# Graph network with capsule routing on one core: shares ahead of the messages, flags in PSUM, half sums on GpSimd and two alternating sum buffers in routing rounds 2 to 6

## The reference

```
xk = normalize(x.reshape(n, 8, 16))          # 8 capsules of 16 features, each to length 1
z = xk[src]                                  # for every edge
u = xk
for _ in range(6):
    p = softmax(sum(z * u[trg], axis=2), axis=1)       # 8 shares of each edge
    agg = segment_sum(z * p[:, :, None], trg, n)
    u = normalize(agg.reshape(n, 8, 16) + xk)
```

## Time and profile before

| what | value |
|---|---|
| median of 3 runs | 12146.04 us (12140.96 to 12165.63) |
| the profiled execution | 12153.88 us |
| its span | 12152.0 us |
| TensorE, weight loads | 57% and 43% of the span busy |
| VectorE | 58% |
| ScalarE | 28% |
| GpSimd | 46% |
| mean granted TensorE clock | 0.713 of full speed |

### The profile page before, as it was taken

One profiled execution on the slowest core, in us unless ns is written; L12 is line 12 of the kernel. 1 busy time (PEld: TensorE's weight loads), 2 busy tenths in 40 slices (PEclk: granted clock), 3 DMA queues, 4 the chain that ended last, 5 costly groups with the idle time before them and its releaser, 6 DMA issues. The chain is left out here.

```text
span 12152.0 us, 198157 instructions
## 1 busy us (share of the span) xinstructions
PE 6929.4 (57%) x41381; PEld 5175.5 (43%) x41382; DVE 7092.0 (58%) x19002; ACT 3369.7 (28%) x10770; POOL 5647.4 (46%) x5161
## 2 busy tenths in 40 slices
PE   4444433333366666787455553555547777777775
PEld 3211112222222222444344442444437676767675
DVE  7422235454554544777544445444448888888888
ACT  0000000000100000121111111333337776777775
POOL 0466656666255554333355553555543343434342
PEclk9767765555655555998655555666669999999998
DMA  0222234444355556554122222333345454545454
GB/s 21 79 105 107 112 95 104 103 105 102 72 156 155 154 155 144 186 180 131 45 58 58 58 58 47 95 97 95 96 86 164 143 163 142 164 143 163 143 163 122
DMA packets 1108605, 1387.92 MB, mean 114 GB/s; under 512 B 277722, under 2 KB 974382, under 8 KB 1108142
## 3 DMA queue, kind: packets, MB, share of 16 engines
q1 hardware_dynamic: 955182, 1090.46, 28.7%
q0 software_dynamic: 153344, 296.65, 11.9%
HBM read 1002.58 MB, written 383.96 MB: 114 GB/s over the span
## 5 line engine op out<-in xcount | busy, mean ns | idle before, releaser
L2097 POOL TENSOR_TENSOR msg_r<-zo_r,ex_r 128x1024 f32<-128x1024 f32 x580 | 1121.6, 1934 | 1878.2 <-ACT ex_r L2184 1878.2
L2192 ACT ACTIVATE hots_r<-zo_r,tot_r 128x128 f32<-128x128 uint8 x4640 | 1416.5, 387 | 576.0 <-DVE tot_r L2137 389.4
L2225 PE MATMUL ps<-msg_r,hots_r 128*128 128x128 f32 x9280 | 1195.2, 282 | 573.9 <-ACT hots_r L2192 461.4
L2225 PEld LDWEIGHTS ps<-msg_r,hots_r 128*128 128x128 f32 x9280 | 1087.6, 193 | 681.5 <-DVE u_sum L2150 666.5
L598 POOL DMA_INDIRECT ring_e<-t_tab,st_e x880 | 831.1, 944 | 893.5 <-DVE st_e L590 597.2
L2213 PE MATMUL ps<-u,wide_r 128*128 x9280 | 1143.2, 277 | 169.2 <-ACT wide_r L2177 164.8
L1879 POOL DMA_INDIRECT z_r<-x_tab,st_r x880 | 833.9, 948 | 808.3 <-issue 441.2
L477 POOL DMA_INDIRECT rec_tab<-st_pay,st_row x832 | 808.6, 972 | 858.3 <-DVE st_pay L529 596.7
L2213 PEld LDWEIGHTS ps<-u,wide_r 128*128 128x128 f32 x9280 | 1093.8, 194 | 171.8 <-issue 171.7
L1078 POOL DMA_INDIRECT ring_m<-t_tab,st_m x880 | 842.8, 958 | 684.9 <-issue 349.4
L598 POOL DMA_INDIRECT ring<-y_tab,st x880 | 883.4, 1004 | 550.5 <-DVE st L590 290.4
(11 more groups left out here) (316 smaller groups left out, 13040.7 us busy)
## 6 DMA issues: line engine op xcount, KB each, us to landing
zo_r<-zo_tab SPq DMA_DIRECT2D x2320, 192.0 KB, 2.6
y_tab<-y_out SPq DMA_DIRECT2D x250, 512.0 KB
k_tab<-ring_m SPq DMA_DIRECT2D x220, 520.0 KB
ring_e<-k_tab SPq DMA_DIRECT2D x220, 520.0 KB
ohts_e<-oht_tab SPq DMA_DIRECT2D x440, 128.0 KB
zo_tab<-z_r SPq DMA_DIRECT2D x220, 256.0 KB
dl_b<-dl_tab SPq DMA_DIRECT2D x220, 128.0 KB
oht_tab<-ohts SPq DMA_DIRECT2D x220, 128.0 KB
```

Of the source, the lines that this page charges most:

```text
L2097: nc.gpsimd.tensor_tensor(msg[:, s % WR].rearrange("p c (k d) -> p c k d", d=CD), z_of(s).rearrange("p c (k d) -> p c k d", d=CD), ex[:, s ...
L2192: last = nc.scalar.activation(hots[:, s % WR, c, :], rows[:, c, :], ACT.Copy, scale=tot[:, s, c:c + 1])
L2225: last = nc.tensor.matmul(ps[:, 4 + s % 2, c // 2 * D:(c // 2 + 1) * D], hots[:, s % WR, c, :], msg[:, s % WR, c, :], start=c % 2 == 0, st ...
```

## The change

In later_rounds, and with small edits around it:

1. **Shares ahead of the messages.** VectorE multiplies the flagged reciprocal with the exponentials into a new tensor share; GpSimd's message multiplies z with it, and waits for it. The one-hot is no longer scaled: hot is one ScalarE instruction over all eight chunks, and waits for nothing of VectorE.
2. **Flags in PSUM.** pair_ok is copied once to PSUM banks 6 and 7. The flagged reciprocal is made from there, and written there.
3. **Half sums on GpSimd.** After the product GpSimd adds features 8 to 15 of each capsule to features 0 to 7 (fold); VectorE's reduction then reads 8 instead of 16 features.
4. **Two sum buffers.** u_sums takes turns by the round. The one not in use is reset to unit by ScalarE in ten pieces during octets 4 to 13. Both are first filled in round 1. u_sq is gone: squares are written into u. y_row and dl_f are freed ahead of the routing layer.
5. **The end of a round in parts**: squares and their sums in four parts, root, maximum, reciprocal and product in two. The first two wide matrices of a round are made in the round before.
6. **Orders.** VectorE, ScalarE, TensorE and GpSimd have new orders, zo has 6 buffers, dot, ex and tot two. SP no longer waits for widen.
7. **No loops**: all 580 octets are written out on every engine, waits are for constants, and 16 register reads stand ahead of every fourth octet.

```
                 OC = 2 * OP
-                WR = 2
+                ZR, WR = 6, 2
+                parts = [(0, 13), (13, 26), (26, 38), (38, NTP)]
...
+                    flat = ps[:, 6:8, :].rearrange("p b w -> p (b w)")
+                    RESETS = 10
+                    def inverse(g):
+                        at = 2 * NPAIR + g % 2 * OC
+                        return flat[:, at:at + OC]
...
+                    def sums_of(r):
+                        return u_sums[(r + 1) % 2]
...
+                            for g in range(rounds * NO):
+                                o = g % NO
+                                if o % 4 == 0:
+                                    places = registers([mybir.EngineType.SP], pair_at, o, NCH - 2)
+                                if g >= ZR:
+                                    sp.wait_ge(s_msg, g - ZR + 1)
+                                    sp.wait_ge(s_hot, g - ZR + 1)
...
+                            def message(g):
+                                pool.wait_ge(s_share, g + 1)
+                                if g >= WR:
+                                    pool.wait_ge(s_sum, g - 1)
+                                nc.gpsimd.tensor_tensor(
+                                    msg[:, g % WR].rearrange("p c (k d) -> p c k d", d=CD),
+                                    z_of(g).rearrange("p c (k d) -> p c k d", d=CD),
+                                    share[:, g % 2, :].rearrange("p (c k) -> p c k", k=CAPS).unsqueeze(3)
+                                    .broadcast_to([P, OC, CAPS, CD]), ALU.mult).then_inc(s_msg, 1)
+
+                            def fold(g):
+                                pool.wait_ge(s_prod, g + 1)
+                                nc.gpsimd.tensor_tensor(prod[:, :, 0:CD // 2], prod[:, :, 0:CD // 2],
+                                                        prod[:, :, CD // 2:CD], ALU.add).then_inc(s_half, 1)
+                            for r in range(rounds):
+                                for k in range(-1, NO + 1):
+                                    if k >= 1:
+                                        message(r * NO + k - 1)
+                                    if k + 1 < NO:
+                                        fold(r * NO + k + 1)
...
+                            def reduce(g):
+                                dve.wait_ge(s_half, g + 1)
+                                if g >= 2:
+                                    dve.wait_ge(s_e, g - 1)
+                                v.tensor_reduce(dot[:, g % 2, :], prod[:, :, 0:CD // 2], AX.X, ALU.add).then_inc(s_dot, 1)
...
+                            def flagged(g):
+                                dve.wait_ge(s_p, 3 * g + 2)
+                                at = g % NO * OC
+                                v.tensor_tensor(inverse(g), flat[:, at:at + OC], tot[:, g % 2, :], ALU.mult)\
+                                 .then_inc(s_p, 1)
+
+                            def shares(g):
+                                dve.wait_ge(s_p, 3 * g + 3)
+                                if g >= 2:
+                                    dve.wait_ge(s_msg, g - 1)
+                                v.tensor_tensor(share[:, g % 2, :].rearrange("p (c k) -> p c k", k=CAPS),
+                                                inverse(g).unsqueeze(2).broadcast_to([P, OC, CAPS]),
+                                                ex[:, g % 2, :].rearrange("p (c k) -> p c k", k=CAPS), ALU.mult)\
+                                 .then_inc(s_share, 1)
...
+                                    if now:
+                                        reduce(g)
+                                    if r >= 1 and k == 2:
+                                        dve.wait_ge(s_u, r * RESETS)
+                                    if behind:
+                                        add(r, late, 0)
+                                    if k + 1 < NO:
+                                        product(g + 1)
+                                    if behind:
+                                        add(r, late, 1)
+                                    if now:
+                                        total_share(g)
+                                    if behind:
+                                        add(r, late, 2)
+                                    if now:
+                                        share_inverse(g)
+                                    if behind:
+                                        add(r, late, 3)
+                                    if now:
+                                        flagged(g)
+                                        shares(g)
...
+                                for n, (a, b) in enumerate([(parts[0][0], parts[1][1]), (parts[2][0], parts[3][1])]):
+                                    dve.wait_ge(s_rt, 2 * r + n + 1)
+                                    link(v.tensor_scalar(norms(a, b), norms(a, b), 1e-12, None, ALU.max))
+                                    link(v.reciprocal(norms(a, b), norms(a, b)))
+                                    v.tensor_tensor(capsules(u, a, b), capsules(sums_of(r), a, b),
+                                                    norms(a, b).unsqueeze(2).broadcast_to([P, (b - a) * CAPS, CD]),
+                                                    ALU.mult).then_inc(s_go, 1)
...
-                                    for c in range(OC):
-                                        last = nc.scalar.activation(hots[:, s % WR, c, :], rows[:, c, :], ACT.Copy,
-                                                                    scale=tot[:, s, c:c + 1])
-                                    last.then_inc(s_hot, 1)
...
+                            def hot(g):
+                                if g >= WR:
+                                    act.wait_ge(s_sum, g - 1)
+                                nc.scalar.activation(hots[:, g % WR], hot_bytes(g, False), ACT.Copy).then_inc(s_hot, 1)
...
+                                for k in range(NO):
+                                    g = r * NO + k
+                                    exponential(g)
+                                    if k + 3 < NO or (k + 3 < NO + 2 and r + 1 < rounds):
+                                        widen(g + 3)
+                                    hot(g)
+                                    if 4 <= k < 4 + RESETS and r + 1 < rounds:
+                                        reset(r, k - 4)
...
+                                for k in range(-2, NO + 1):
+                                    g = r * NO + k
+                                    if k + 2 < NO:
+                                        if (k + 2) % 4 == 0:
+                                            tiles = registers(PE_ENGINE, pair_tile, k + 2, NT)
+                                        expand(g + 2, tiles)
+                                    if k >= 1:
+                                        total(g - 1)
```

More of the change, by code:

```diff
@@ new lines, in norms, with capsules, registers @@
+                    def norms(a, b):
+                        return nrm[:, a * CAPS:b * CAPS]
+                    def capsules(big, a, b):
+                        return big[:, a:b, :].rearrange("p t (k c) -> p (t k) c", c=CD)
+                    def registers(engine, table, o, most):
+                        return nc.values_load_multi_w_load_instructions(
+                            table[0:1, o * OP:min(o + 4, NO) * OP], engines=engine, min_val=0, max_val=most,
+                            skip_runtime_bounds_check_because="a bucket or a chunk number, bounded where the table is made")[1]
@@ new lines, in _ @@
+                            for r in range(rounds):
+                                if r >= 1:
+                                    pe.wait_ge(s_go, 2 * r)
+                                for k in range(-2, NO + 1):
[6 more added lines that the diff above has]
+                                        total(g - 1)
```

276 lines of the change are left out of this document (120 added, 156 removed).

## The result

| kernel | median, us | lowest to highest | runs |
|---|---|---|---|
| before | 12152.43 | 12140.96 to 12165.63 | 4 |
| changed | 11515.24 | 11509.13 to 11551.14 | 4 |

What follows compares the result with a forecast made beforehand. VectorE bounds the kernel at 4.81 us an octet; TensorE would then set 3.95. Octets save 494.5 us, round boundaries 45, entry to round 2 0.5: 540 less, 11606 us on the median's scale, range 11490 to 11848.

Steps and rivals of the forecast that it cites:

- the prediction's own signs of being wrong: In the trace: VectorE's waits before the reduction naming GpSimd, TensorE waiting on messages, or issue gaps every few octets.
- its first case: Routing octets: TensorE sets the period, 3.75 to 4.15 us, total 11490 to 11720 us; chance 0.70.
- TensorE's octet, 3.84: Routing octet on TensorE: the same matmuls, 4.66 less 0.82 idle, need 3.84 us.
- T = 3.80 + 0.15: Octet period: TensorE's matmuls plus its register reads, no longer under idle time, give 3.95 us.
- VectorE then wants 3.6 to 3.8: VectorE's octet after the change: 3.58 us plus up to 0.20 of register reads, at worst 3.95.
- nothing else needs as much: Routing octets: no other engine needs as much time as TensorE, so TensorE sets the period.
- Six buffers in place of four ... Nothing: Source loads by DMA: two more buffers give one or two octets of lead, no time gained.
- (a): Rival, octet loop: a cross-engine chain of message, half sum, reduction and shares sets 4.2 to 4.6 us; chance 0.22.
- the margin of 0.3: GpSimd's half sum ends at 3.3 us of VectorE's step, covered by 0.3 or more before the next reduction.
- about 21: Between routing rounds: TensorE idles about 21 us.
- (b): Rival, written-out octets: instruction fetching stalls engines; 1.1 us an octet would give 12238 us; chance 0.04.
- (c): Rival, flags' multiplication: its 0.5 us is not GpSimd's hold, so nothing gained, 12130 to 12187 us; chance 0.04.

Runs made afterwards that it cites:

- e3: Changed kernel without register reads on VectorE, bucket sums going to fixed, wrong rows: 11386.74 us, ratio 0.9384 to the kernel before.
- e4: Changed kernel with VectorE's register reads moved from ahead of the reduction to behind the product of the octet before: 11400.37 us, ratio 0.94 to the kernel before.
- e11: Changed kernel with VectorE's register reads behind the product, e4's edit again on another chip: 10392.63 us, 118 less than e10.
- e9: Changed kernel with VectorE's order of operations as in the kernel before: 10623.16 us, 112 more than e10.
- e1: Changed kernel with the flags' multiplication reading the flags from SBUF again, output still in PSUM: 11592.63 us, 77 more than the changed kernel.
- e2: Changed kernel without half sums on GpSimd, VectorE's reduction reading all 16 features: 11726.27 us, 211 more than the changed kernel.
- e8: Changed kernel with four zo source buffers in place of six: 12433.06 us, ratio 1.1169 to the kernel before, 1922 us more than e10.
- e12: Changed kernel with five zo source buffers in place of six: 10572.66 us, 62 more than e10.
- e7: Kernel before with one edit, the flags copied to PSUM once and multiplied from there: 10999.92 us, ratio 0.9882 to the kernel before.
- e10: Changed kernel itself, run again on the third chip: 10510.83 us, ratio 0.9441 to the kernel before.

## Why the prediction was right, and where it was off

**Right in sign and in the means, not in the bound.** VectorE was the bound at 4.81; the hold by GpSimd, the order, the half sums and the round's end all showed, and TensorE ended near full. The period came out 3.79 for 3.95: 575 x 0.16 = 92 of the 97 us by which the forecast of the saving was short. But TensorE alone does not set this period, and two of the prediction's own signs of being wrong stood in the trace: "issue" gaps every four octets (141.8 us) and TensorE waiting on messages (103.9). That the period still fell into the band of its first case, 3.75 to 4.15, is in part luck: TensorE's octet was taken 0.38 too long, and 0.22 of waiting for each other, which the sum did not have, made up for over half of it.

**The mis-sized term is TensorE's octet, 3.84, and with it "T = 3.80 + 0.15".** It measured 3.57. The working added 1.89 (one group's start to the next) to 1.95 (the next group's record to its end, taken from an octet in which TensorE idled behind it). Back to back both groups step by 1.79. Of the difference 0.16 is the overlap of a record's end with the next start; 0.10 is that a group behind an idle takes longer, as again here, where the sums at 9616.49 are 1.89 long to the next start. The text gave "some 0.1 less", it is 0.27. The 0.15 for TensorE's register reads was nothing: with them it is busy 99.8% of e3's stretch.

**What set 3.79 are VectorE and TensorE by turns, through a term that the text had and did not use.** "VectorE then wants 3.6 to 3.8" was 3.58 + 0.20. Measured are 3.42 + 1.03/4 = 3.68, above TensorE's 3.57 and below the period. The remaining 0.11 is VectorE waiting for the sums of a TensorE that its own read had held up: in four octets the read takes 1.03 us from VectorE, the message is late by it, TensorE loses 0.77 ahead of the sums and 0.10 in them, and 14.28 + 0.87 = 15.15, against the 15.12 of four periods. VectorE, faster than TensorE by 0.15 an octet, catches up and waits in its turn. The read was taken at the 0.8 us of the earlier trace rows's wait and is 1.0. So "nothing else needs as much" was the false sentence. Shown by e3, e4 and e11: without the exposed reads TensorE's 3.57 to 3.59 is the period and 115 to 129 us go.

**VectorE's parts.** Step 3.58 forecast, 3.42 measured. Flags 165 ns (0.20 to 0.27 as a step), shares 225, reduction 686 for 678, neighbouring sums apart: all as costed. As shares of the time they were worth less alone than in the sum, as leaving one out shows: half sums 211, order 112 (net of the reads that e9 hides), flags 77, round ends 39, shares 17, together 456 of 637. Why the rest belongs to no part alone was not taken apart. One reason shows in e1 and e2: what a part fails to save goes first into the waits for TensorE's sums, 0.11 an octet.

**"Six buffers in place of four ... Nothing" was wrong as a step.** It was read as more lead for a wait of 121.6 us. In the new order of ScalarE it decides over more than the whole gain: 1922 us without it (e8), 62 with one buffer of two (e12). The forecast did not suffer, because the change has both. What was missed is a ring through load, widen and hot; the ring examined under (a) left the loads out.

**GpSimd.** Half sum 1.27 for 1.0 to 1.2. The prediction's estimate of 1.11 us from the figure in section 3.1 of the Trainium skill's page GPSIMD Engine Reference is low as well; 1266 ns for 512 elements is more an element than the message's 1934 for 1024. By the list of waits it stayed covered, with 14.1 us of idle ahead of the reduction in all. By the starts the margin of 0.3 is gone: the half sum ends at 9613.10 + 1.27 = 9614.37, and the reduction starts at 9614.40, 0.20 behind the shares' start where e1 and e2 have 0.15. So in these octets the reduction seems to wait 0.05 for it, under the record of the shares.

**Round ends.** 45 forecast; 39 by leaving them out, and 22.1 us of idle for "about 21". A round took 10018.60 - 9546.41 = 472.2 us for the 487 forecast; 115 x 3.79 = 436 of it, so 36 for boundary and filling, against 34.

**The rivals.** (a), T 4.2 to 4.6, did not happen. Its mark, TensorE waiting on messages, showed (103.9 us), but e4 removed most of it by moving reads alone: it followed from them. (b): instructions are fetched in 387 packets, 4.6 MB, for 79 packets before, and TensorE and VectorE show no gap for it: TensorE's 99.8% in e3 leaves none. By the rule of the Trainium skill's page Runtime: NRT & Kernel Launch, section Instruction fetch mechanics, straight code is fetched ahead; the trace agrees. (c), that the hold is something else, is refuted by e1: with the input back in SBUF, and the output still in PSUM, the multiplication ends 0.03 us behind GpSimd's instruction. The share multiplication was not held (225 ns). The DMA share was 0.70 for 0.65, of which the shorter period makes 0.68.

**Left open.** What limits e7 at 4.58 us (300/65.5) was not taken apart: by its waits it is a ring over scaled copies, TensorE and loads, but no run separated them. Nor was it tried whether the order of before, exponential and widen behind hot, would let the changed kernel do with four buffers.

## What to carry to other kernels

Take an engine's floor from start to start of groups that stand back to back, never as a record's length, and compare all engines' floors with their periodic extras (here 1.0 us of register reads per four octets) before naming the next bound. Where two floors are close, as 3.57 and 3.68 here, the period can be longer than both (3.79), since each engine hands its hold-ups to the other. When an order is changed, draw each ring through the buffers, the loads included: a buffer that is freed behind an instruction that waits for a load sets how many are needed. Put register reads behind a long instruction of their engine: behind 1.22 us they cost VectorE nearly nothing, behind 0.69 us (e9) 0.38.

## What was not expected of the hardware

- A VectorE multiplication of 8 elements, both inputs in SBUF, waits for GpSimd's whole instruction: means of 671 ns beside the 1.93 us message and 397 beside the 1.27 us half sum (e1), for 165 with one input in PSUM. The product and the sums, which read one input from PSUM, keep 1220 and 288 ns beside both. The Trainium skill's page SBUF — State Buffer, section SBUF: two separate sides, states such an exclusive hold; the trace agrees for VectorE's side.
- Reads of sixteen values into registers cost VectorE 1.0 us in the open. Issued behind an instruction of 1.22 us they nearly disappear (e4, e11), and on TensorE, behind 16 matmuls, too (e3).
- The kernel before took 1000 us less on two of the chips. In the changed kernel the difference lies ahead of round 2, and the change saves 637 us in the slower setting and 623 in the faster. GpSimd's indirect loads in round 1 have the same length on both. They span 1498 us in the changed kernel's first profile and 1156 in e10's, and start 660 us later in the first (line, instructions: duration ns min/median/max, first and last start):

```profile
L1881 POOL DMA_INDIRECT z_r<-x_tab,st_r x880: 938/944/1449, 7547.0 to 9044.8; - x176
```

```profile
L1881 POOL DMA_INDIRECT z_r<-x_tab,st_r x880: 938/944/1437, 6886.9 to 8042.9; - x176
```

The first row is from the changed kernel's first profile, the second from e10. Why the transfers behind them differ was not studied.
